# First layer's receptance: mixed tokens into one matmul, in place of two matmuls with mixed weights

## The reference, cut to what matters

```python
x_prev = jnp.pad(x[:, :-1, :], ((0, 0), (1, 0), (0, 0)))
xk = x * time_mix_k + x_prev * (1.0 - time_mix_k)
xv = x * time_mix_v + x_prev * (1.0 - time_mix_v)
xr = x * time_mix_r + x_prev * (1.0 - time_mix_r)
k = jnp.einsum('bth,oh->bto', xk, W_k)
v = jnp.einsum('bth,oh->bto', xv, W_v)
r = jax.nn.sigmoid(jnp.einsum('bth,oh->bto', xr, W_r))
wkv = _wkv_full(k, v, time_decay, time_first)      # a scan over the 256 tokens
out = jnp.einsum('bth,oh->bto', r * wkv, W_o)
```

## Time and profile before

| | |
|---|---|
| device time, median of 3 runs | 1105.07 us (1103.41 to 1105.41) |
| the profiled execution's own time | 1104.67 us |
| its span, from first to last instruction | 1102.9 us |
| first layer | from 0 to about 358 us of the span |
| steps 11 to 34 (experts and recurrent work together) | from about 170.6 to 347 us |
| PE / DVE / ACT / POOL busy, share of the span | 89 / 84 / 74 / 65% |

### The profile page before, as it was taken

The page is one execution under the profiler, slowest core; times in us unless marked ns, Lnnn a source line. Parts: engine busy times, 40 slices in busy tenths (PEclk is TensorE's granted clock), DMA queues, the critical chain, the costliest instruction groups (busy, mean ns, idle before and its releaser), DMA issues.

```text
span 1102.9 us, 28968 instructions
## 1 busy us (share of the span) xinstructions
PE 978.7 (89%) x9146; PEld 681.3 (62%) x9146; DVE 926.9 (84%) x2016; ACT 814.8 (74%) x1984; POOL 721.8 (65%) x1035
## 2 busy tenths in 40 slices
PE   2576537999998589999999999999999999999996
PEld 2455427999997356666666666666666666666653
DVE  6769997999998479888888888888888888888782
ACT  2456425877775358888888888888888888888884
POOL 4476777778888466666676667666766676666431
PEclk9766668999999679999999999999999999999998
DMA  9511115555553433233323332333333333333310
GB/s 256 126 37 40 40 37 146 166 163 160 164 155 113 99 80 97 77 85 94 95 77 86 99 89 76 92 95 88 77 98 87 88 79 97 96 78 76 91 42 17
DMA packets 157438, 106.42 MB, mean 96 GB/s; under 512 B 72745, under 2 KB 137449, under 8 KB 157161
## 3 DMA queue, kind: packets, MB, share of 16 engines
q1 hardware_dynamic: 153192, 96.05, 33.4%
q0 software_dynamic: 4096, 8.53, 2.6%
HBM read 72.95 MB, written 31.47 MB: 95 GB/s over the span
## 4 chain that ended last, share of the span: by engine, by line
PE 59%; issue 4%; POOL 2%; DVE 1%; SPq 1%; DMA 0%; ACT 0%; POOLq 0%
PE PS L1973 10%; PE PS L1928 6%; PE PS L2021 6%; PE PS L1950 6%; PE PS L2076 5%; PE PS L2051 5%; PE PS L2094 5%; PE PS L2036 4%; PE PS L1906 3%; PE PS L2104 3%; PE PS L1989 2%; PE PS L2008 2%; PE PS L1894 1%; DVE bm L1599 1%; PE PS L2102 1%
## 5 line engine op out<-in xcount | busy, mean ns | idle before, releaser
L1599 DVE TENSOR_REDUCE bm<-PS 128x16 f32<-128x1024 f32 x256 | 311.6, 1217 | 74.2 <-PE PS L1928 72.7
L1818 ACT ACTIVATE PT<-PS 128x1024 f32<-128x1024 f32 x256 | 261.7, 1024 | 59.7 <-PE PS L1950 59.6
L1483 POOL TENSOR_TENSOR Pr<-Pr,linv 128x512 f32<-128x512 f32 x128 | 131.7, 1040 | 65.1 <-DVE linv L1626 63.3
L1973 PE MATMUL PS<-PT,rows 128*32 128x256 f32 x2048 | 136.4, 384 | 0.1
L1791 ACT ACTIVATE Pr<-PS,nmf 128x256 f32<-128x256 f32 x256 | 117.0, 470 | 4.6 <-DVE nmf L1619 4.6
L1928 PE MATMUL PS<-KS,QS 48*128 48x256 bf16 x1024 | 101.3, 276 | 7.7 <-DVE bm L1599 5.3
L1950 PE MATMUL PS<-QS,KS 51*128 51x256 bf16 x1024 | 99.6, 272 | 3.4 <-ACT PT L1818 1.6
L474 POOL DMA_INDIRECT xs_dram<-rows,slot x64 | 65.6, 1025 | 38.8 <-DVEq L703 21.1
L1008 PE MATMUL PS<-S,wmix 128*128 128x256 f32 x192 | 69.0, 446 | 19.3 <-DVE diff L731 18.3
L1973 PEld LDWEIGHTS PS<-PT,rows 128*32 128x32 f32 x2048 | 57.2, 109 | 46.3 <-issue 18.3
L1619 DVE TENSOR_REDUCE nmf<-PS 128x4 f32<-128x1024 f32 x64 | 78.0, 1219 | 7.8 <-PE PS L2051 7.8
(11 more groups left out here) (251 smaller groups left out, 2473.0 us busy)
## 6 DMA issues: line engine op xcount, KB each, us to landing
up<-in_up_w SPq DMA_DIRECT2D x72, 256.0 KB, 3.2
wsel<-in_qkv_w SPq DMA_DIRECT2D x128, 96.0 KB, 2.5
parts_dram<-parts SPq DMA_DIRECT2D x32, 384.0 KB, 2.6
QS<-parts_dram SPq DMA_DIRECT2D x64, 96.0 KB
KS<-parts_dram SPq DMA_DIRECT2D x64, 96.0 KB
xs_dram<-zero_t SPq DMA_DIRECT2D x1, 4752.0 KB, 26.6
xs_t<-xs_dram SPq DMA_DIRECT2D x24, 198.0 KB, 2.8
ys_dram<-ys_t SPq DMA_DIRECT2D x24, 192.0 KB
```

The source lines that it names most:

```text
L1483: pool.tensor_tensor(Pr[i][:, qt, :, :], Pr[i][:, qt, :, :], linv[:, i, qt, :].unsqueeze(2).broadcast_to([P, 2, SEQ]), ALU.mult).then_inc( ...
L1599: dve.tensor_reduce(bm[:, i // 2, :, 2 * (i % 2):2 * (i % 2) + 2, :].rearrange("p q r b -> p r q b"), bS.rearrange("p (r q b k) -> p r q b ...
L1818: act.activation(PT[i % 4][:, :, :], shifted_bank(t, i).rearrange("p (r k) -> p r k", r=2), ACT.Exp).then_inc(s_exp, 1)
L1973: last = pe.matmul(b_values_out[u][j * VC:(j + 1) * VC, 0:SEQ], V2[t % NQ][:, kt, :, :].rearrange("p h c -> p (h c)")[:, at:at + VC], PT[( ...
```

## The change

ACT scales the tokens by `time_mix_r` into a tile `now`, and their predecessors by `1 - time_mix_r`, one column further, into a tile `then`, whose first column is zero. POOL adds the two in place. PE does one matmul of the unscaled weights over the sum. For sequence t the ACT part lies in step t + 2, between `expert_out` and `copy_tokens` (before the exponentials in steps below 11), the POOL part at the head of step t + 3, before everything else that POOL does in it, and the matmul where it was, in step t + 4. DVE no longer makes the two scaled matrices of r in `setup` and zeroes two columns in their place. All 32 sequences are done so.

```diff
+        now, then = two("mixed_now", [P, SEQ]), two("mixed_before", [P, SEQ])
...
+            def mix(t, q):
+                pool.wait_ge(s_mx, t + 1)
+                pool.tensor_tensor(now[q % 2][:, :], now[q % 2][:, :], then[q % 2][:, :], ALU.add).then_inc(s_mix, 1)
...
                 w, m, d = (lag(quad, p, k) for k in (3, 4, 5))
+                if runs(w[0]):
+                    mix(*w)
                 if s in (FIRST + 1, FIRST + 2, FIRST + 3):
                     constants(s - FIRST - 1)
...
-                for j in range(3):
+                for i in range(2):
+                    dve.memset(then[i][:, 0:1], 0.0)
+                for j in range(2):
...
+            def mix_tokens(t, q):
+                if t == 0:
+                    act.wait_ge(s_setv, 2)
+                act.wait_ge(s_xnT, t + 1)
+                after(act, s_rp, t - 1)
+                act.activation(now[q % 2][:, :], xnT(t), ACT.Identity, scale=cols[:, 4:5])
+                act.activation(then[q % 2][:, 1:SEQ], xnT(t)[:, 0:SEQ - 1], ACT.Identity, scale=ommix[:, 2:3]).then_inc(s_mx, 1)
...
+                x = lag(quad, p, 2)
...
                     expert_out(group(s, 2))
                 take(2)
+                if runs(x[0]):
+                    mix_tokens(*x)
                 if s < FIRST and runs(e[0]):
                     exps(*e)
...
             def receptance(t, q):
                 pe.wait_ge(s_kv, most(t + 3))
-                project(t, 2, psR, s_rp)
+                pe.wait_ge(s_mix, t + 1)
+                pe.matmul(psR, w0[:, 2, :], now[q % 2][:, :], start=True, stop=True).then_inc(s_rp, 1)
```

More of the change, by code:

```diff
@@ L304, in layer_zero @@
         s_kv = sem("values_ready")
+        s_mx = sem("r_parts_scaled")
+        s_mix = sem("r_tokens_mixed")
         s_rp = sem("r_in_psum")
```

## The result

| | before | after |
|---|---|---|
| median (lowest to highest) of 11 executions each | 1103.5 us (1101.68 to 1107.52) | 1107.32 us (1105.5 to 1111.13) |
| the profiled execution's own time, its span | 1104.67, 1102.9 us | 1109.57, 1107.8 us |
| last quarter's first scatter | 140.72 | 142.29 |
| SP issues the experts' first load | 166.57 | 169.35 |
| first `scale_tokens` | 170.59 | 171.95 |

The change made the kernel slower by 0.29%: the ratio is 1.0029, with an interval of 1.0017 to 1.0041. That is 1.9 to 4.5 us, most likely 3.2.

The account below looks back on a forecast made before the run. PE paces the regular expert steps; DVE, then POOL's queue, set the scatter stretch's end. Terms -1.0 + 4.5 + 1.0 = +4.5 us on 1104.67 gave 1109.2, or 1109.6 on the median; range 1101 to 1113.

Parts of the forecast that it names:

- Regular steps: 19 expert steps from 188.94 to 331.23 us: each goes from 7.38 to 7.33 us, 1.0 us gained (0 to 2.1).
- Both loops: Regular steps: a loop through ACT of 7.27 us and one through POOL and DVE of 7.32 to 7.38, just under 7.38.
- Scatter stretch: Additions hold DVE 0.7 us longer: five in full 3.5, the first 0.35, one on POOL's own path 0.7; 4.5 us lost.
- (b): Rival: DVE gets in between weigh and addition; scatter stretch loses 2.8 us, regular steps gain 1.0 to 2.1; 1106.3 us; chance 0.18.
- PE in the scatter stretch: Intake and scatter stretch: PE waits for DVE anyway, so the saved matmul counts nothing there.
- Experts' start: Sign that the forecast is right: the first expert instruction on ACT comes near 175 us instead of 170.6.
- moved by less than 2 us: Sign that the forecast is wrong: the experts' start moves by less than 2 us.
- Steps at the start: Two steps at the experts' start: one matmul less, two ACT instructions more, -0.9 to +0.8 us; taken as 0.
- The last steps: Last expert steps, 314.6 to 346.8 us, with five additions: between 0 and 3.5 us lost; taken as 1.0.
- the clock: PE, granted 1.00 (2.4 GHz) where busy for 29.1 of 32.2 us, should keep it when idling some per cent.
- (a): Rival: additions don't hold DVE; scatter stretch loses only 0.7 us; time 1103.7 down to 1099.1 us; chance 0.17.
- (c): Rival: POOL's loop outgrows the present step; regular steps lose 1.9 us, last 3.5, scatter stretch 4.9; 1115.4 us; chance 0.10.

Follow-up runs that it names:

- e3: Changed kernel without ACT's scaling: the single matmul and POOL's addition, of tiles that stay zero; 1107.3 us, ratio 1.0041 to the kernel before.
- e4: Kernel before, keeping its two matmuls, with POOL's addition of two constant tiles put in, nobody waiting for it; 1109.47 us, ratio 1.0051.
- e9: e7_up_first with ACT's two scalings moved behind copy_tokens from step 11 on; 1107.57 us, ratio 1.0029 to the kernel before.
- e1_pe_only: Changed kernel with the single matmul alone, over unmixed tokens, without ACT's scaling and POOL's addition; 1099.04 us, ratio 0.9959 to the kernel before.
- e2_pe_act: Changed kernel without POOL's addition: the single matmul and ACT's scalings stay; 1100.3 us, ratio 0.9963 to the kernel before.
- e10_late: The change made only for sequences from 8 on, additions beginning in step 11, behind the last scatter; 1105.43 us, ratio 1.0014 to the kernel before.
- e8_old_up_first: Kernel before with SP's loads of expert weights issued ahead of the store and load that wait for POOL's skip; 1102.61 us, ratio 0.9979.
- e5: Kernel before with a POOL fill of 128x768 elements, which only writes, in the place of e4's addition; 1107.76 us, ratio 1.0026.
- e12_dve_mix_up_first: e11_dve_mix with SP's loads of expert weights ahead of the store and load; 1117.36 us, ratio 1.0118 to the kernel before.
- e13_mid_step: Changed kernel with POOL's addition moved from the step's head to between the products and divide; 1107.17 us, ratio 1.0036 to the kernel before.
- e7_up_first: Changed kernel with SP's loads of expert weights issued ahead of the store and load that wait for POOL's skip; 1107.74 us, ratio 1.0026 to before.
- e11_dve_mix: Changed kernel with one DVE instruction scaling the tokens and adding the predecessors, nothing new on POOL; 1118.01 us, ratio 1.0112 to the kernel before.

## Why the prediction was right, and where its terms were off

The side was right, and so was the main mechanism: the additions hold DVE, in the scatter stretch and in the steps, and PE's saving doesn't come through. That the size came so near is in part luck, since terms that were too high and too low by 1 to 2 us each cancel, as shown below. The forecast was +4.5 us; measured are 3.2 (1.9 to 4.5). The absolute time lies 2.3 us under the forecast, of which 1.6 is that the kernel before took 1103.5 beside it, not 1105.07.

**Regular steps, forecast -1.0 us over 19.** Both loops are there: 7.27 foretold by way of ACT, 7.28 measured; 7.32 to 7.38 by way of POOL, 7.24 measured in e3, e4 and e9. The second is no floor for a single step, as e3's steps of 6.99 show, only for many. What failed is the step from loops to a sum. I multiplied the ordinary step by 19, but the 19 of the earlier trace rows were not all ordinary: 142.3 us are 7.49 each, 14 of them 7.37 or 7.38 and five 7.47 to 8.60, and the last of them lie in the stretch from 314.6 us that I counted again. After the change nine of the 12 regular steps last 7.27 or 7.28 us and three 7.37, 7.68 and 8.55. Twelve of 7.28 would have won 1.2 us; the three are 1.76 over that; the sum is 0.56 lost. Over the prediction's 19 steps it is 334.01 - 190.34 = 143.67, against 142.29, 1.4 lost. In the step of 8.55 us the inner passes wait for DVE, in the timeline of the kernel after:

```profile
287.20 0.95 DVE L796 SCALAR_TENSOR_TENSOR rows<-rows 128x256 f32<-128x256 f32 x1
...
294.32 0.96 DVE L771 TENSOR_TENSOR expert_work<-PS,expert_work 128x768 f32<-128x768 f32 x1
295.38 2.92 PE L1070 MATMUL PS<-xsT,up 128*128 128x128 f32 x24 [1.32 <-DVE expert_work L771]
```

L796 belongs to the second layer and takes 0.95 us of DVE; the kernel before has it too (L785, at 285.83) and its step stays 7.38, because DVE still had 1.27 us in hand there; here it had 0.33. The steps of 7.68 and 7.37 are steps with late weights (24 passes in 3.34 and 3.03 us instead of 2.94).

**Scatter stretch, forecast +4.5 us.** For the additions alone this was nearly right. In e4_old_pool the last quarter starts 143.57 - 140.72 = 2.85 us later (I had 3.85), and SP's load is issued 170.63 - 166.57 = 4.06 us later. The addition on POOL's own path cost 0.86 rather than 0.7 between the two halves of the scatters (15.34 us against 155.20 - 140.72 = 14.48), and from there to SP's load it is 0.35 more (11.72 against 11.37), which I had not counted. Each of the six in front cost 0.48 on average, since DVE mostly gets in between, as rival (b) had it: in five of the six in e4 a DVE instruction held by `weigh` got in as the addition began, and the next one then waited instead (L636's kind took 0.80 us, 0.28 alone). The kernel before had shown this too: at 153.40, which the prediction counts among six like cases, L741 had got in between `divide` and `weigh` (1.15 us from 152.84), and L361 then waited for `weigh` (1.42 us from 153.91). Once in the six DVE was kept out to the end of the addition in the kernel after. The same stretch of the kernel before, DVE and POOL:

```profile
91.92 2.62 DVE L636 SCALAR_TENSOR_TENSOR xn_sq<-xn_sq,minus_scale_sq 128x128 f32<-128x128 f32 x1
92.42 0.74 POOL L486 TENSOR_TENSOR rwkv<-num,den 128x256 f32<-128x256 f32 x1
93.10 1.28 POOL L480 TENSOR_TENSOR ev<-ex,values 128x512 f32<-128x512 f32 x1
```

And of the kernel after:

```profile
91.27 3.29 DVE L647 SCALAR_TENSOR_TENSOR xn_sq<-xn_sq,minus_scale_sq 128x128 f32<-128x128 f32 x1
91.77 0.74 POOL L493 TENSOR_TENSOR rwkv<-num,den 128x256 f32<-128x256 f32 x1
92.45 1.27 POOL L483 TENSOR_TENSOR ev<-ex,values 128x512 f32<-128x512 f32 x1
93.68 0.72 POOL L488 TENSOR_TENSOR mixed_now<-mixed_now,mixed_before 128x256 f32<-128x256 f32 x1
```

A DVE instruction that takes 0.28 us alone stands until the third POOL instruction is over, 0.67 us longer than before, which is the 0.7 of the prediction.

**PE in the scatter stretch, counted as nothing.** This was wrong. With the single matmul the load comes 0.8 us earlier (e1_pe_only), with ACT's part 1.7 (e2_pe_act). PE's receptance lies ahead of the ranks for which DVE waits: 5.07 us before, 2.45 after, at this row of the kernel after:

```profile
72.48 0.29 DVE L688 COPY tot<-PS 128x128 f32<-128x128 f32 x1 [2.45 <-PE PS L1026]
```

In the kernel before the same copy starts at 74.02. These are differences of single profiles: e10_late, with the same matmuls as before in this stretch, repeats the load to 0.2 us (166.37), and e8_old_up_first, with a stall of 2.71 us, is 0.74 later. Why ACT's part should bring it another 0.9 us forward isn't shown. "PE waits for DVE anyway" held on average and not at the place where DVE waits for PE. With both parts: 4.06 - 1.66 = 2.4, and 169.35 - 166.57 = 2.78 us were measured at the load.

**Experts' start, forecast near 175, measured 171.95.** The first load and the first `scale_tokens` of the kernel after:

```profile
169.35 0.91 SPq L402 DMA_DIRECT2D xs_t<-xs_dram  x2
171.95 0.98 ACT L910 ACTIVATE expert_work<-xs_t 128x128 f32<-128x128 f32 x3 [5.25 <-DMA xs_t<-xs_dram]
```

The kernel before issues the same load at 166.57. From issue to ACT it is 2.60 us after and 4.02 before, so half of the delay of 2.78 is given back here, and nothing in the prediction foresaw that. By the letter of the prediction "moved by less than 2 us" is a sign against it; the delay was there, 2.6 us upstream of the mark that I had chosen.

**Steps at the start, forecast 0:** from `scale_tokens` to the first of the 12 steps 48.65 us before and 48.22 after, -0.4.

**The last steps, forecast +1.0, and the clock, forecast 1.00.** The five steps cost 2.77 us more. About half of it is the clock. The windows of the kernel after:

```profile
342.00:344.00 2.00, 0.44 (x3) 0.47 (x4) 1.97 (x3) 1.97 (x5) 1.92 (x4) 0.94 0.68 225
344.00:346.00 2.00, 2.00 (x11) 2.00 (x11) 2.00 (x2) 0.81 (x1) 2.00 (x3) 0.50 0.14 42
346.00:348.00 2.00, 2.00 (x15) 2.00 (x14) 1.97 (x3) 0.00 (x0) 1.37 (x2) 0.71 0.78 191
```

And its timeline, the inner matmuls there:

```profile
343.56 4.54 PE L1070 MATMUL PS<-xsT,up 128*128 128x128 f32 x24 [2.57 <-DMA up<-in_up_w]
```

PE had waited 2.57 us and was then granted 0.50, the level of 1.2 GHz, for some 3 us. The 24 passes take 4.54 us, in place of 2.94 elsewhere and of 3.44, with late weights, in the same step of the kernel before: 1.1 to 1.6 us. In the forecast, PE was to keep its clock there; the row that it rested on is the mean of a stretch in which no wait was this long. Between 211 and 314 us the clock was 1.00, as forecast.

The sum by the profiles: +2.78 to the load, -1.42 in its landing, -0.43 + 0.56 + 2.77 in the steps, and from there to the second layer 13.52 after and 13.95 before, -0.43. That is +3.83, as 364.53 - 360.70. Against the forecast the load came 1.7 us less late, the landing and the two ends gave back 2.3 that stood in no term, and the steps lost 3.0 more: 0.56 instead of a gain of 0.6 in the 12, and 2.77 instead of 1.0 in the five. By parts, from the medians: the single matmul gives 4.6 us (1103.61 - 1099.04), ACT's part takes back 1.3 (1100.3 - 1099.04), the addition 7.0 (1107.32 - 1100.3; the kernel before took 1103.5 and 1103.61 beside these two).

Of the rivals, (a) fell with e4 and e5 (the addition does hold DVE), (c) in size. (b) described rightly how most of the additions meet DVE. Its 2.8 us for the scatter stretch is the measured 2.78 by luck: the additions alone cost 4.06 (e4), and the difference is PE's saving, which (b) didn't count either. Its gain of 1 to 2 us in the steps didn't come.

## What to carry to other kernels

An engine at 100% covers the uneven moments of the one behind it; before taking work off it, read that one's busy share (here DVE, 95%) and take the mean of many steps, not the best one. A limit that lies under the present step still costs time when it uses up the margin out of which uneven moments were paid: here DVE's 7.24 us under PE's 7.38. An instruction added to POOL is not free because POOL idles: in this kernel 0.73 us of tensor addition cost DVE 0.3 to 0.4 us in each step (0.33 in the kernel after, 0.32 from e1 to e3, 0.44 from before to e4) and up to 0.7 in the scatter stretch, while a fill of the same length left the same DVE instruction as it was. Where a stretch waits for a chain of two engines, count a saving on either of them at the very instruction at which the other waits.

## What the runs showed that was not expected

- **DVE is kept out over three POOL instructions in a row**, 3.29 us for an instruction of 0.28, and at other times it gets in between two of them, and then POOL's second takes 0.96 instead of 0.73. The Trainium skill, SBUF — State Buffer, section Who interferes with whom, speaks of an exclusive lock, held for a whole instruction; read strictly, this would let DVE in each time. The trace shows both courses. RECIPROCAL, which reads one SBUF tile, stays at 1.74 us beside any of them.
- **PE's clock after a wait in the last steps.** It fell to 0.50 after waits of 2.27 us (e12_dve_mix_up_first), 2.40 (e10_late), 2.43 (e2_pe_act), 2.57 (after), 2.71 (e13_mid_step) and 1.85 (e3_pe_pool, e7_up_first), and the 24 inner passes then took 4.16 to 4.58 us in place of 2.9 to 3.2. It stayed at 1.00 after 1.84 (e9_both), 1.76 (e1_pe_only), 1.47 (e4_old_pool) and less, but also after 2.63 us in e11_dve_mix, so the length of the wait alone doesn't decide it. The timeline of e11_dve_mix:

```profile
355.06 2.92 PE L1071 MATMUL PS<-xsT,up 128*128 128x128 f32 x24 [2.63 <-DMA up<-in_up_w]
```

- **The experts' first load lands in 4.0 or in 2.6 us.** It took 4.02 us from issue to ACT in the kernel before and 4.21 in e8_old_up_first, and 2.59 to 3.02 in all twelve profiles of kernels that have the two new tiles. Why is open.
- **A stall of DVE and ACT together** near 106 us. The timeline of the kernel after:

```profile
106.00 0.29 DVE L688 COPY tot<-PS 128x128 f32<-128x128 f32 x1 [2.97 <-remote]
106.05 0.37 ACT L866 COPY S<-PS 128x256 f32<-128x256 f32 x1 [2.64 <-remote]
```

It is also in the profiles of e5_old_pool_fill (3.12), e7_up_first (1.45) and e8_old_up_first (2.71 on DVE), the last with the code of the kernel before in this stretch. ACT alone has one of 2.05 us in e9_both at 104.09, and there is none in those of before, of e1_pe_only to e4_old_pool and of e10_late to e13_mid_step. So it isn't the change's doing, but it blurs a comparison of single profiles. Its cause is open.
